# A gated delta-rule block on one core: first and last heads in an order of their own, the output product in pieces, k and q norms from transposes

## The reference, cut to what matters

```python
x = x + 0.5 * ffn(layernorm(x))
x = x + attn(layernorm(x))
x = x + 0.5 * ffn(layernorm(x))
# attn, 16 heads of 128:
q, k, v = (silu(short_conv(x @ W.T)) ...)          # causal, 4 taps
v_hat = k @ Wsv.T; e = v_hat - v                    # s = (|e|_2, |e|_1, 1 - cos(v_hat, v))
beta, amp = sigmoid(mlp_b(s)), mlp_a(s)
g = -exp(A_log) * softplus(k / |k| * amp + dt_bias)
qn, kn = q / sqrt(sum(q*q) + eps), k / sqrt(sum(k*k) + eps)
# step: S = S * exp(g); delta = (v - kn.S) * beta; S += kn delta; o = (qn * scale).S
o = o * rsqrt(mean(o*o) + eps) * norm_w * sigmoid(gate)
return o @ Wo.T
# ffn, 16 experts, top 4 of a softmax, and a shared one twice as wide:
y = sum_e combine[e] * (silu(x @ w_gate[e]) * (x @ w_up[e])) @ w_down[e] + shared
```

## Time and profile before

| what | us |
|---|---|
| median of 3 runs | 1904.7 |
| lowest and highest | 1889.76 and 1914.15 |
| the profiled execution | 1899.87 |
| its span, first to last instruction | 1898.1 |

### The profile page before, as it was taken

The page is one execution under the profiler, slowest core; times in us unless marked ns, Lnnn a source line. Parts: engine busy times, 40 slices in busy tenths (PEclk is TensorE's granted clock), DMA queues, the critical chain, the costliest instruction groups (busy, mean ns, idle before and its releaser), DMA issues.

```text
span 1898.1 us, 27509 instructions
## 1 busy us (share of the span) xinstructions
PE 1711.0 (90%) x9800; PEld 1373.3 (72%) x9800; DVE 1087.4 (57%) x1828; ACT 816.8 (43%) x1630; POOL 513.4 (27%) x802
## 2 busy tenths in 40 slices
PE   6999998658999999999999999999887439999999
PEld 4777775346887788788878887888876338777776
DVE  2322222357898898888888988998662102322222
ACT  2222223343456546545654664556332760322222
POOL 1000000014354435544544544444443000000000
PEclk9999999677899999999999999999887769999999
DMA  8000000001112011201210121111011801100000
GB/s 284 1 1 1 1 1 1 9 9 34 27 36 60 15 56 49 59 13 47 59 52 21 46 60 26 46 39 51 14 48 40 336 0 45 47 1 1 1 6 17
DMA packets 121558, 78.71 MB, mean 41 GB/s; under 512 B 55952, under 2 KB 109904, under 8 KB 120656
## 3 DMA queue, kind: packets, MB, share of 16 engines
q1 hardware_dynamic: 120384, 76.93, 13.4%
q10 hardware_dynamic: 1040, 0.02, 0.0%
HBM read 56.48 MB, written 20.46 MB: 41 GB/s over the span
## 4 chain that ended last, share of the span: by engine, by line
PE 82%; DVE 7%; ACT 6%; issue 4%; ACTq 1%; POOL 1%; DVEq 0%; POOLq 0%
PE proj L345 18%; PE bank L867 10%; PE proj L753 10%; PE bank L369 9%; PE bank L891 4%; PE bank L899 3%; PE bank L1051 3%; PE proj L796 2%; DVE front L1359 2%; PE bank L909 2%; PE bank L953 2%; PE proj L786 2%; ACT L1274 2%; PE bank L850 1%; PE bank L924 1%
## 5 line engine op out<-in xcount | busy, mean ns | idle before, releaser
L588 DVE SCALAR_TENSOR_TENSOR front<-proj,comb,front 128x176 f32<-128x176 f32 x288 | 115.4, 401 | 434.9 <-ACT front L432 434.9
L867 PE MATMUL bank<-KQ,front 128*128 128x128 f32 x1792 | 252.7, 298 | 18.4 <-POOL front L1697 6.0
L867 PEld LDWEIGHTS bank<-KQ,front 128*128 128x128 f32 x1792 | 237.1, 210 | 33.1 <-issue 25.4
L432 ACT ACTIVATE front<-proj 128x176 f32<-128x176 f32 x288 | 91.3, 317 | 347.0 <-PE proj L345 346.8
L1359 DVE SCALAR_TENSOR_TENSOR front<-proj,pall,front 128x1022 f32<-128x1022 f32 x144 | 184.1, 1279 | 78.8 <-ACT front L1077 41.4
L345 PE MATMUL proj<-back,xT 128*128 128x352 f32 x640 | 219.3, 466 | 3.4 <-ACT xT L424 3.4
L753 PE MATMUL proj<-xT,wqkv 128*128 128x512 f32 x384 | 188.4, 636 | 19.9 <-DVE front L1359 16.6
L1695 POOL TENSOR_TENSOR front<-front 128x512 f32<-128x512 f32 (+6 forms) x112 | 85.3, 761 | 366.4 <-PE bank L867 366.4
L345 PE MATMUL proj<-front,xT 128*128 128x352 f32 x512 | 172.6, 460 | 0.0
L1516 DVE TENSOR_TENSOR KQ<-KQ,front 128x1024 f32<-128x1024 f32 x112 | 160.9, 1436 | 7.2 <-PE bank L867 5.2
L1697 POOL TENSOR_TENSOR front<-front 128x512 f32<-128x512 f32 x112 | 149.2, 1332 | 0.0
(11 more groups left out here) (182 smaller groups left out, 3116.3 us busy)
## 6 DMA issues: line engine op xcount, KB each, us to landing
m_img<-back SPq DMA_DIRECT2D x16, 512.0 KB, 3.2
inv<-t_img SPq DMA_DIRECT2D x16, 512.0 KB, 4.1
back<-t_img SPq DMA_DIRECT2D x16, 512.0 KB, 5.4
o_scr<-obuf SPq DMA_DIRECT2D x15, 512.0 KB, 6.2
front<-o_scr SPq DMA_DIRECT2D x3, 2560.0 KB, 16.5
back<-in_w_gu SPq DMA_DIRECT2D x20, 352.0 KB, 9.7
wqkv<-in_wqkv SPq DMA_DIRECT2D x16, 384.0 KB, 5.7
front<-in_w_gu SPq DMA_DIRECT2D x16, 352.0 KB, 12.4
```

The source lines that it names most:

```text
L432: se.activation(sg[:, i % 2, :], bank[i % 2][:, 0:INTER], ACT.Silu).then_inc(f_sg, 1)
L588: ve.scalar_tensor_tensor(act[:, u % 2, e * INTER:(e + 1) * INTER], bank[i % 2][:, INTER:2 * INTER], comb[:, n, at:at + 1], sg[:, i % 2, : ...
L867: m = te.matmul(dst, suf[:, c * P:(c + 1) * P], right, start=True, stop=True)
```

## The change

The loop of turns runs from 3 to 14 on each engine. Ahead of it stands a list begin(), behind it a list finish(), written out step by step for each engine. In the loop most steps have another place; levels 2 to 6 of a head now follow in one turn, and on ACT there are three changes to each table set per turn. The norms of k and q are taken from transposes (into FF) that ACT squares 128 columns at a time with a running sum. The diagonal is written after level 0. The output product is cut into pieces of one head and four row blocks, with cleared banks 0 to 3, placed between steps of heads 14 and 15 and behind them. Its inputs are loaded in four groups as buffers come free, and wo lies elsewhere. The store of W and of its transpose, and the two loads from there, are separate steps.

```diff
-FIRST, LAST = 0, NH + 13
+FIRST, LAST = 3, 15
-        o_all = front[:, :].rearrange("p (h t) -> p h t", h=NH)
+        wo = cut(5120, 4096).rearrange("p (h d) -> p h d", d=H)
+        def o_rows(h):
+            return inv[:, (h - 5) * TOK:(h - 4) * TOK] if 5 <= h < 9 else front[:, h * TOK:(h + 1) * TOK]
...
-                sy.dma_start(weights_of(g, e), a["w_gu"][e0 + e]).then_inc(s_fw[(e0 + e) // 2], 16)
+                sy.dma_start(weights_of(g, e), a["w_gu"][e0 + e]).then_inc(s_fw[(e0 + e) // 4], 16)
...
                 if i >= 2:
                     te.wait_ge(f_act, f * PAIRS + i - 1)
+                elif f:
+                    te.wait_ge(x_up, 5 + i)
...
-            ve.tensor_tensor(rows, rows, bank[4 + q], ALU.add).then_inc(x_up, 1)
+            ve.tensor_tensor(rows, rows, bank[q], ALU.add).then_inc(x_up, 1)
...
+            def t_out_w(h):
+                sy.wait_ge(*sub.of(h, 2 * SUB - 1))
...
+            def wo_load():
+                sy.wait_ge(*red_.of(end))
+                sy.dma_start(wo, a["WoT"]).then_inc(s_wo, 16)
+            def o_load_a():
+                sy.wait_ge(*kq.of(end))
+                sy.wait_ge(*dg[0].of(end))
+                sy.wait_ge(*dg[1].of(end))
+                o_load(0, 5, s_oa)
+            def o_load_b():
+                sy.wait_ge(*tt6.of(end))
+                o_load(5, 9, s_ob)
...
             def p_k(h):
-                te.wait_ge(*rts_.of(h - 1))
+                te.wait_ge(*ksq.of(h - 1))
...
-            def p_norms(h):
-                te.wait_ge(*ksq.of(h))
+            def to_rows(v, done):
+                for c in range(BN):
+                    m = te.transpose(FF[:, c // NC, c % NC * P:(c % NC + 1) * P], v[:, c * P:(c + 1) * P], ident[:, :])
+                m.then_inc(done.sem, 1)
+            def p_kk(h):
+                te.wait_ge(*silu.of(h, 1))
                 te.wait_ge(*prod.of(h))
-                for j, v in enumerate((t1, gx)):
...
+                to_rows(cvk[:, h % 2, :], kk)
+            def p_qq(h):
+                te.wait_ge(*silu.of(h, 3))
+                te.wait_ge(*ksq.of(h, 1))
+                to_rows(cvq[:, h % 2, :], kk)
...
             def t_diag(h, b):
-                te.wait_ge(*kn[b].of(h))
+                te.wait_ge(*put[b].of(h, 1))
                 te.wait_ge(*silu.of(h, 3))
-                te.wait_ge(*kTs[b].of(h - 1))
...
+            def o_part(h, lo, hi):
+                te.wait_ge(wo_s, 2)
+                if h < 5:
+                    te.wait_ge(s_oa, 16 * 5)
...
+                for n in range(lo, hi):
+                    o_block(n, h, False)
+            def o_last(q):
+                te.wait_ge(*fin[q // 2].of(end))
+                for n in (2 * q, 2 * q + 1):
+                    m = o_block(n, end, True)
+                m.then_inc(wo_mm, 1)
...
+            def finish():
...
+                c_u(14, 0, 2)
+                c_u(14, 1, 2)
+                o_part(0, 0, 4)
+                c_ko(14, 0, 2)
+                c_ko(14, 1, 2)
+                o_part(1, 0, 4)
+                c_p(14, 1, 3)
+                c_p(14, 0, 3)
+                t_lvl(15, 1, 5)
+                o_part(2, 0, 4)
...
+                c_ko(15, 1, 3)
+                c_ko(15, 0, 3)
+                o_part(5, 0, 4)
...
+                c_oT(15, 0)
+                o_zero(2)
+                o_zero(3)
+                o_part(0, 4, 8)
...
+                o_last(0)
+                o_last(1)
+                o_last(2)
+                o_last(3)
...
             def k_sq(h):
-                se.wait_ge(*silu.of(h, 1))
+                se.wait_ge(*kk.of(h, 1))
+                se.wait_ge(*rts_.of(h - 1))
                 se.wait_ge(*ss.of(h - 1))
-                se.activation(t1, cvk[:, h % 2, :], ACT.Square).then_inc(ksq.sem, 1)
+                for c in range(BN):
+                    m = se.activation(t1[:, c * P:(c + 1) * P], FF[:, c // NC, c % NC * P:(c % NC + 1) * P], ACT.Square,
+                                      accum_out=kq2[:, 0, c:c + 1])
+                m.then_inc(ksq.sem, 1)
...
-                ve.tensor_tensor(AM[:, h % 2, b, :, 1, :], L[b].rearrange("p (n v) -> p n v", n=NC),
-                                 ident[:, :].unsqueeze(1).to_broadcast([P, NC, P]), ALU.mult).then_inc(putd[b].sem, 1)
+                ve.copy_predicated(AM[:, h % 2, b, :, 1, :], dmask[:, :].unsqueeze(1).to_broadcast([P, NC, P]),
+                                   L[b].rearrange("p (n v) -> p n v", n=NC)).then_inc(putd[b].sem, 1)
...
+                if l == 0:
+                    ve.wait_ge(s_mo, 16 * (h - 1) if h > 1 else 0)
+                    ve.wait_ge(*ko[b].of(h - 2))
+                    ve.tensor_tensor(pairs(AM[:, h % 2, b, :, :, :].rearrange("p n q v -> p (n q) v"), 0)[:, :, :, 1, 0],
+                                     L[b].rearrange("p (a m) -> p a m", a=2 * NC),
+                                     fmask[:, :].unsqueeze(1).to_broadcast([P, 2 * NC, HALF]), ALU.mult).then_inc(put[b].sem, 1)
...
                 if l:
                     ge.wait_ge(*mdec.of(h, l))
                     ge.wait_ge(*msuf.of(h, l))
+                else:
+                    ge.wait_ge(*dg[0].of(h))
+                    ge.wait_ge(*dg[1].of(h))
```

More of the change, by code:

```diff
@@ L716, in spill, with o_load @@
                     sy.dma_start(o_scr[h], obuf[:, :]).then_inc(s_o, 16)
-            def turn(t):
-                m_in(t - 11)
-                t_out(t - 11)
-                t_in(t - 11)
-                spill(t - 13)
-                gate_weights(t - 11)
-                weights(t - 7)
-                m_out(t - 10)
+            end = NH - 1
+            def wo_load():
+                sy.wait_ge(*red_.of(end))
+                sy.dma_start(wo, a["WoT"]).then_inc(s_wo, 16)
+            def o_load(first, last, done):
+                sy.wait_ge(s_o, 16 * last)
+                for h in range(first, last):
+                    m = sy.dma_start(o_rows(h), o_scr[h])
+                    m.then_inc(done, 16)
@@ L868, in t_lvl, with t_diag @@
                 m.then_inc(lvl[b].sem, 1)
+            @live
+            def t_diag(h, b):
+                te.wait_ge(*put[b].of(h, 1))
+                te.wait_ge(*silu.of(h, 3))
+                for n in range(NC):
+                    c = b * NC + n
+                    m = te.matmul(L[b][:, n * P:(n + 1) * P], suf[:, c * P:(c + 1) * P], cvq[:, h % 2, c * P:(c + 1) * P],
+                                  start=True, stop=True)
+                m.then_inc(dg[b].sem, 1)
             @live
@@ new lines, in begin @@
+            def begin():
+                p_k(0)
+                p_v(0)
+                p_q(0)
+                p_vT(0)
+                p_vhat(0)
+                p_kk(0)
+                p_qq(0)
+                p_k(1)
+                g_sT(0)
+                g_hid(0)
+                g_z(0)
+                p_v(1)
+                g_amp(0, 0)
+                g_amp(0, 1)
+                p_q(1)
+                p_vT(1)
+                p_vhat(1)
+                g_norm(0, 0)
+                g_norm(0, 1)
+                p_kk(1)
+                t_lvl(0, 1, 0)
+                t_lvl(0, 0, 0)
+                p_qq(1)
+                t_diag(0, 1)
+                t_diag(0, 0)
+                p_k(2)
+                t_lvl(0, 1, 1)
+                t_lvl(0, 0, 1)
@@ L1057, in attention_se @@
+            te.wait_ge(*kTs[1].of(end))
+            te.wait_ge(*tt6.of(end))
         def attention_se(se):
@@ L1339, in attention_se @@
+            begin()
             for t in range(FIRST, LAST):
                 turn(t)
[L1341 to L1344 removed]
+            finish()
         def attention_ve(ve):
```

1586 lines of the change are left out of this document (1349 added, 237 removed).

## The result

The changed kernel takes 1838.7 us (median of 4 runs, 1835.1 to 1844.2), the kernel before 1901.0 us on the same chip: ratio 0.967 with a 95% interval of 0.960 to 0.974. The profiled execution is 1837.8 us with a span of 1836.0. So 62 us were gained where 112 were forecast; the time lies just inside the range. The slices of the page, against the earlier trace rows: the low clock at the end of attention is gone; the one at its start is not.

A forecast was written before the change was run, and what follows sets the result against it. PE's own work was taken to bound the steady turns, one head's chain the start and end. Savings of 10 (start) + 33 (turns) + 69 (tail) = 112 us gave 1788, 1792 in the median's terms; range 1750 to 1842.

The forecast's parts named there:

- the turns: Twelve steady attention turns, p_k(3) to p_k(15): from 64.54 to 61.8 us each, 33 us saved.
- rival 1: Steady turns gain nothing because DVE or the squares' path ends last: 79 us saved, 1825 us; chance 0.20.
- The wait: PE's 47.49 us before the output product, laid to ACT's 36 empty-turn table loads (46.4 us), which go.
- (a): Tail, from p_k(15) to level 0 of head 15: 116 us taken in place of 123.9.
- (b): Tail, from head 15's level 0 to its last state step: 88 us taken in place of 91.5.
- (c): Tail, the output product's remaining 108 blocks with last transposes and clearing matmuls: 50.4 us.
- (d): Tail, time given back as norms are exposed after the product: 7.5 plus about 1.5 us, less 2.6.
- 5 + 5: Saving taken for the start, the first heads before the steady turns: 10 us, bounds 20 saved and 6 lost.
- Rival 2: Transposes let the clock fall like the one-column passes: turns of 63.05 us, 1807 us; chance 0.08.
- Rival 3: New order also closes gaps in turns and start: turns of 60.0 us, 1762 us; chance 0.13.
- Rival 4: Squares cost near a whole one each, PE waits for banks: turns of 73.7 us, 1936 us; chance 0.04.
- rival 5: The product's first piece waits for late o_scr loads, delaying head 15's state steps 10 us: 1802 us; counted within the forecast.

The follow-up runs named there:

- e4_loads: Kernel before with ACT's loop ended at its last live turn, so without the 36 table loads of empty turns: 1860.1 us.
- e12_sums: Changed kernel with the old norms put back (squares of 1024 columns, sixteen one-column sums in one block): 1923.5 us.
- e1_split: Changed kernel with GpSimd's substitution cut in two and level 5's t_dec placed between the parts: 1895.5 us.
- e3_norms: Kernel before with the new norms alone (transposes and squares of 128 with sums, no column sums): 1920.1 us.
- e8_ring: Changed kernel, steady turns reordered so less stands between the first inverse product of level 4 and the store of the low levels: 1865.5 us.
- e10_soft: Changed kernel with VectorE's soft_low and soft_relu moved behind taps_q in the 12 steady turns, away from GpSimd's substitution: 1832.3 us.
- e11_clear: Changed kernel with soft_low, soft_relu and also the multiplication by level 5's decay moved behind taps_q on VectorE: 1847.3 us.
- e9_short: Changed kernel with the last seven of fifteen steps of GpSimd's substitution left out, so part of the inverse isn't computed: 1801.6 us.

## Why the prediction was right or wrong

**The total.** 1.6 us from the start, -20.2 from the turns, 81.6 from the tail and -1.2 from the last part give 61.8 us, where 10 + 33 + 69 were forecast. The time is inside the range by 3 us, and only because the range was drawn past rival 1: the tail's unforeseen 13 us made good a part of what the turns lost. That is luck, and no sign that the turns were understood.

**The wait, right.** No table loads in a row are left and the product waits for nothing. e4_loads puts 35 us on it by itself.

**The tail, right in kind, 13 us better.** (a) 110.5 us for the 116 taken, (b) 85.1 for 88, (c) 49.2 for 50.4, (d) 3.4 us and a wait of 0.9 us behind it for the 6.4 of 7.5 + 1.5 - 2.6. The seam, PE of the kernel after:

```profile
1542.07 0.63 PE L331 MATMUL bank<-ident,KQ 128*128 128x128 f32 x4 [2.06 <-DVE KQ L533]
1543.42 1.42 PE L355 MATMUL proj<-back,xT 128*128 128x352 f32 x4 [0.72 <-issue]
1548.30 1.45 PE L355 MATMUL proj<-back,xT 128*128 128x352 f32 x4 [0.94 <-DVE front L600]
```

The exposed norm shows as waits of 2.06 and 0.94 us. The first pair's statistics run beside the last product blocks. Tail in all: 82 us saved, 69 forecast.

**The start, wrong by its only unsupported number.** p_k(2) starts at 432.12 instead of 433.93; 1.6 us are saved, not 10. The "5 + 5" had no row behind it. PE's waits there are for the filter taps and ACT's copies (5.15 and 4.06 us in a row), and the new order leaves them.

**The turns, wrong, and the reason for the missing 50 us.** 33 us were to be saved and 20 were lost. The priced terms were right: two groups of transposes take 1.03 us each; the clock behind them is 1.00 where it was 0.52; a turn's PE work came out at 59.6 us (22.67 + 36.95), against 61.8 less the idle 1.9 of before; ACT's turn is 40.9 us for the 40.4 taken. The squares stay hidden. ACT's groups by form in the kernel after (busy, mean ns):

```profile
L1735 ACT ACTIVATE front<-proj 128x128 f32<-128x128 f32 x128 | 33.5, 294 | 17.4 <-PE proj L996 17.4
L1735 ACT ACTIVATION_READ_ACCUMULATOR front<-proj 128x1 f32 x128 | 28.9, 226 | 0.0
```

and the window of the second transposes of a turn and t_diag behind them:

```profile
959.10:962.50 3.40, 3.40 (x27) 2.92 (x26) 3.38 (x3) 2.18 (x16) 0.41 (x1) 1.00 0.02 5
```

A square of 128 is 0.294 us and a read of its sum 0.226, and they overlap: eight of each take 2.18 us in the window above, by the estimate of 0.268 each 2.1.

What failed is the sentence "Most of the other reordering within a turn I cost at nothing: PE's work is the same", and under it the reading "the steady turns are PE's own work". PE was busy 97% of a turn that two stretches made up, each at its own limit: stretch 1 was as long as store, substitution and load (28.5 us) and happened to be filled to 27.1. Work taken out of it gave nothing back. The reordering moved 5.4 us from it into stretch 2, which ate the 1.5 us of the norms and the better clock; in exchange PE got an idle 4.7 us. Time added to stretch 2 is paid in full: PE is busy 4.2 us more in it in e12_sums and 3.0 in e1_split, and it is 4.5 and 2.7 us longer. That the turn would be shorter by as much with these steps back in stretch 1 is not shown: no run puts them there without other moves, and in e3_norms and e8_ring stretch 2 stayed at 37.2 and 36.9 us with 4 and 3 us of it idle on PE. On top, the substitution takes 14.3 us for 12.5 because other VectorE operations now run beside it, as e10_soft and e11_clear show. That ate what the change won by waiting for one load: the load lands 28.1 us behind the store in the mean, for 28.4 of the later of two before.

**The rivals.** Rival 1's number (1825) came nearest, but not its mechanism: neither VectorE's share nor the squares end the turn. Rival 2 is out by the clock above. Rival 3 is out: closed gaps were not to be had. Rival 4's exposure of the squares did not come; rival 5's loads were not waited for. What I had of the true mechanism was one clause, that GpSimd is busy only 31.8 us a turn, "which hides it". A busy share says nothing about a queue that is on the path for 14 us of each turn.

**Left open.** How much of stretch 1's 28.8 us PE's order behind level 6 holds alone: the load by itself holds 28.1. What sets stretch 2 at about 37 us when PE has less to do in it was read from waits (GpSimd's t_dec, VectorE's masks) and not tested by a run. Whether an order exists with the tail of the changed kernel and turns of 64.5 us or less wasn't settled; e8_ring was one try.

## What to carry to other kernels

An engine that is busy 97% of a steady loop needn't set it. Draw the loop's ring first, from one head's store to the next through every queue and transfer, and split the turn where the path changes hands: an engine's time can be a gain only where it is taken out of a stretch that this engine fills, and even there only down to the next chain's length (e3_norms, e8_ring). A step moved over such a border can have a price though the sum of work is the same. Price an edit in the order that it will run in: the same norms were worth minus 25 us in one order and plus 85 in the other.

## What the runs showed of the hardware

GpSimd slows down beside some VectorE operations and not beside others. Timelines of GpSimd and VectorE in the kernel after:

```profile
928.57 1.19 POOL L2906 TENSOR_TENSOR W<-W,prodw 64x64 f32<-64x64 f32 x1
929.83 0.30 POOL L2903 TENSOR_TENSOR prodw<-D,W 64x63 f32<-64x63 f32 x1
930.21 0.32 POOL L2906 TENSOR_TENSOR W<-W,prodw 64x63 f32<-64x63 f32 x1
930.61 0.72 POOL L2903 TENSOR_TENSOR prodw<-D,W 64x60 f32<-64x60 f32 x1
...
923.44 3.90 DVE L2262 SCALAR_TENSOR_TENSOR front<-proj,pall,front 128x1022 f32<-128x1022 f32 x3
928.37 1.22 DVE L2416 TENSOR_TENSOR KQ<-KQ,front 128x1024 f32<-128x1024 f32 x1
930.49 0.69 DVE L2380 TENSOR_SCALAR front<-front 128x1024 f32<-128x1024 f32 x1 [0.91 <-ACT front L1781]
```

A subtraction of 64x63 takes 0.32 us at 930.21, where VectorE is idle, one of 64x64 1.19 us beside the 128x1024 tensor_tensor with both inputs in SBUF at 928.37; a product beside the tensor_scalar at 930.49 takes 0.72 instead of 0.30. Beside the filter taps (923.44 to 927.3), which read PSUM, the steps stay at 0.23 to 0.31. The Trainium skill, GPSIMD Engine Reference, Key points, says that GpSimd contends with VectorE instructions in a 2-port mode or with two SBUF inputs; the rows agree for the operation with two SBUF inputs, and for the tensor_scalar they show the slow step but not its mode. Further, e10_soft and e11_clear show that the order decides how often it happens. It goes the other way too: in e9_short, VectorE's eight-column operation for tokf takes 1.86 us beside GpSimd's soft_res, and 0.16 us in the kernel after. The timeline of e9_short:

```profile
914.87 1.86 DVE L2356 TENSOR_TENSOR tokf<-rt,sqb 128x8 f32<-128x8 f32 x1
```

and of the kernel after:

```profile
931.76 0.16 DVE L2356 TENSOR_TENSOR tokf<-rt,sqb 128x8 f32<-128x8 f32 x1
```

A sum taken with an activation shows as an instruction of its own (0.226 us above), but it overlaps with its neighbours: eight squares and eight reads take 2.18 us together, less than the 2.35 us of the eight squares' own times (8 x 0.294).
